# Wide attention of a Perceiver block: keys' high and low parts in tiles of their own, score products in row tiles, four chunks a step

## The reference, cut to what matters

```python
xn = _layernorm(x, ln_gamma, ln_beta)
q = (xn @ w_q).reshape(B, SQ, 16, 64)                 # B=4, SQ=256
k, v = split(context @ w_kv)                          # SK=4096, 16 heads of 64 each
scores = einsum('bqhd,bkhd->bhqk', q * 64**-0.5, k)
attn = softmax(scores, axis=-1)
out = einsum('bhqk,bkhd->bqhd', attn, v).reshape(B, SQ, 1024) @ w_out + b_out
```

## Time and profile before

| | |
|---|---|
| runs | 4200.05, 4213.23, 4216.68 us |
| profiled execution, span | 4206.0 us (the page gives no further time of it; the runs' median is 7.2 us above its span) |
| TensorE busy | 3714.7 us, 88% |
| VectorE, ScalarE, GpSimd busy | 2654.0, 2456.7, 1649.3 us |
| prelude of the wide attention | 73 to about 140 us |
| its loop | about 140 to 2080 us |
| granted TensorE clock | 0.943 of full speed over the span |

### The profile page before, as it was taken

One profiled execution on the slowest core, in us unless ns is written; L12 is line 12 of the kernel. 1 busy time (PEld: TensorE's weight loads), 2 busy tenths in 40 slices (PEclk: granted clock), 3 DMA queues, 4 the chain that ended last, 5 costly groups with the idle time before them and its releaser, 6 DMA issues. The chain is left out here.

```text
span 4206.0 us, 77561 instructions
## 1 busy us (share of the span) xinstructions
PE 3714.7 (88%) x28216; PEld 2624.0 (62%) x28216; DVE 2654.0 (63%) x3564; ACT 2456.7 (58%) x4550; POOL 1649.3 (39%) x1365
## 2 busy tenths in 40 slices
PE   5899999999999999999777895699999987767399
PEld 3677777777777777777454794555555543334298
DVE  4666666666666666666145412477878877467577
ACT  3677777776777777677424111266666666435165
POOL 2566666666666666666502201201111000014033
PEclk9999999999999999999788897799999999879599
DMA  6777677777767766665110384788887844100011
GB/s 217 269 253 248 239 260 257 254 249 257 249 243 256 257 245 224 230 223 211 63 36 6 138 319 168 236 165 179 178 166 178 160 77 65 25 11 1 17 46 44
DMA packets 236312, 727.25 MB, mean 173 GB/s; under 512 B 47884, under 2 KB 133132, under 8 KB 167052
## 3 DMA queue, kind: packets, MB, share of 16 engines
q1 hardware_dynamic: 233248, 713.89, 54.9%
q0 software_dynamic: 2688, 8.39, 0.5%
HBM read 627.80 MB, written 94.37 MB: 172 GB/s over the span
## 5 line engine op out<-in xcount | busy, mean ns | idle before, releaser
L753 POOL TENSOR_TENSOR wa_acc<-wa_acc,wa_probs 128x512 f32<-128x512 f32 x960 | 1246.7, 1299 | 527.8 <-ACT wa_probs L614 447.9
L678 DVE TENSOR_REDUCE wa_mx<-wa_ps_m 128x2 f32<-128x1024 f32 x512 | 626.8, 1224 | 487.2 <-PE wa_ps_m L489 487.1
L614 ACT ACTIVATE wa_probs<-wa_ps_s 128x512 f32<-128x512 f32 x1024 | 556.1, 595 | 530.9 <-PE wa_ps_s L535 525.6
L1292 DVE TENSOR_REDUCE na_mx<-na_ps_m 128x2 f32<-128x1024 f32 x512 | 613.8, 1220 | 196.1 <-PE na_ps_m L1113 192.6
L1237 ACT ACTIVATE na_probs<-na_ps_s 128x512 f32<-128x512 f32 x1024 | 555.8, 595 | 309.9 <-PE na_ps_s L1133 307.6
L606 ACT ACTIVATE wa_ps_s<-wa_m_wide 128x512 f32<-128x512 f32 x1024 | 575.5, 605 | 1.0
L511 PE MATMUL wa_ps_o<-wa_probs,wa_values 128*64 128x256 f32 x4096 | 507.6, 391 | 0.0
L450 PE MATMUL wa_ps_k<-wa_k_ctx,wa_w_k 128*128 128x512 f32 x1488 | 388.8, 397 | 0.0
L476 PE MATMUL wa_ps_v<-wa_w_v,wa_v_ctx 128*128 128x256 f32 x2880 | 383.1, 283 | 0.0
L535 PE MATMUL wa_ps_s<-wa_qh,wa_keys 128*128 128x256 f32 x2048 | 382.2, 309 | 0.0
L511 PEld LDWEIGHTS wa_ps_o<-wa_probs,wa_values 128*64 128x64 f32 x4096 | 275.3, 138 | 149.5 <-issue 7.5
(11 more groups left out here) (341 smaller groups left out, 5382.4 us busy)
## 6 DMA issues: line engine op xcount, KB each, us to landing
wa_k_ctx<-ctx_split SPq DMA_DIRECT2D x248, 1024.0 KB, 5.0
wa_v_ctx<-ctx_split SPq DMA_DIRECT2D x120, 1024.0 KB, 5.6
na_ctx<-ctx_split SPq DMA_DIRECT2D x56, 1024.0 KB, 11.8
na_keys<-k_rows SPq DMA_DIRECT2D x384, 128.0 KB
ctx_split<-wa_stage SPq DMA_DIRECT2D x32, 1024.0 KB, 9.7
wa_land<-in_ctxT SPq DMA_DIRECT2D x32, 512.0 KB, 10.0
ge_w_b<-in_w_rows SPq DMA_DIRECT2D x8, 2048.0 KB, 8.2
k_rows<-na_k_high SPq DMA_DIRECT2D x64, 256.0 KB, 3.3
```

Source lines behind the costliest of these rows:

```text
L614: act.activation(probs[:, c % R:c % R + 2, h * SQ:(h + 1) * SQ], ps_s[n % BANKS][:, :].rearrange("p (c n) -> p c n", c=2), ACT.Exp).then_i ...
L678: dve.tensor_reduce(mx[:, half, :, k], ps_m[:, :, :], AX.X, ALU.max).then_inc(m_taken, 1)
L753: pool.tensor_tensor(acc[:, :], acc[:, :], probs[:, c % R, :], ALU.add).then_inc(summed, 1)
L1292: dve.tensor_reduce(mx[:, half, :, k], ps_m[n % 2][:, :, :], AX.X, ALU.max).then_inc(m_taken, 1)
```

## The change

It touches `wide_attention` alone.

- `keys[i][h]` become `keys_high[i]` and `keys_low[i]`, both heads in their own 64 partitions; `qh` is kept once. `take_keys` is one 128-partition instruction on ScalarE and one on VectorE.
- All score products (low keys x high queries, high keys x high queries, high keys x low queries) are 64-row matmuls, head 0 and head 1 in turn: 24 a step.
- A step `j` is four chunks, eight steps a block. The score banks are four; the values' own bank is gone: in the loop value units go through the banks of the maxima (`ps_m[:, n, :]`), the turned maxima through `ps_m[:, 1, :]`, and in the prelude values go through the score banks.
- `acc` is doubled. `open_banks` comes after the prelude, with float32r matmuls.
- The order in a step is new for all streams:

```diff
+            for j in range(-2, LAST + 1):          # TensorE
+                a, st = j // SS, j % SS
+                of_max, kb, units = max_block(j), key_block(j), value_units(j)
+                if of_max is not None:
+                    pe.wait_ge(v_ready, values_before(j))
+                    if st == 0:
+                        pe.wait_ge(wide_ready, a + 1)
+                    maximum(*of_max, 0)
+                if 0 <= j < LAST:
+                    scores(2 * j)
+                    scores(2 * j + 1)
+                if of_max is not None:
+                    maximum(*of_max, 1)
+                if kb is not None:
+                    project_keys(kb)
+                if st == SS - 1 and a + 1 < G:
+                    pe.wait_ge(m_taken, maxima_through(j))
+                    turn_maximum(a + 1)
+                for n, (q, hb) in enumerate(units):
+                    pe.wait_ge(m_taken, maxima_through(j))
+                    pe.wait_ge(v_ready, values_before(j))
+                    if n and st == SS - 1 and a + 1 < G:
+                        pe.wait_ge(wide_ready, a + 2)
+                    project_values(q, hb, ps_m[:, n, :])
+                if j >= 1:
+                    weigh(j - 1)
+                if st == 0 and j > 0:
+                    denominator(a - 1)
...
+            for j in range(-2, LAST):              # ScalarE
+                turning = st == SS - 1 and a + 1 < G
+                kb = key_block(j)
+                if j >= 0:
+                    for n in range(4):
+                        exponents(4 * j + n)
+                if j >= -1 and not turning:
+                    initial(4 * j + 4)
                 if kb is not None:
                     take_keys(kb)
+                if turning:
+                    take_maximum(a + 1)
+                    initial(4 * j + 4)
+                if j >= -1:
+                    for n in range(1, 4):
+                        initial(4 * j + 4 + n)
+                if j >= 0 and st == 2 and a < BLOCKS - CG:
                     split(a + CG)
...
+            for j in range(-2, LAST + 2):          # VectorE
+                if st == SS - 1 and a + 1 < G:
+                    finish_maximum(a + 1)
+                if st == 1 and j > 1:
+                    copy_out(a - 1)
+                if of_max is not None:
+                    take_maximum(*of_max, 0)
+                    take_maximum(*of_max, 1)
+                if st == 1 and j > 1:
+                    divide(a - 1)
+                if j >= 0 and st == 2 and a < BLOCKS - CG:
+                    split_low(a + CG)
                 if kb is not None:
                     take_keys(kb)
+                for n, (q, hb) in enumerate(value_units(j)):
+                    take_values(q, hb, ps_m[:, n, :])
```

The score products and the schedule of value units:

```diff
             def scores(t):
...
+                    for n, (of, q) in enumerate(((keys_low, qh), (keys_high, qh), (keys_high, ql))):
+                        for h in range(2):
+                            r = slice(h * DH, (h + 1) * DH)
+                            ins = pe.matmul(ps_s[(2 * t + h) % BANKS][:, i * SQ:(i + 1) * SQ], of[a % 2][r, cols], q[a % 3][r, :],
+                                            start=False, stop=(n == 2), skip_group_check=True)
...
+        def max_block(j):
+            n = j + 1
+            return (1 + n // SS, n % SS) if 0 <= n < SS * (G - 1) else None
+        def value_units(j):
+            q, f = (j + 6) // (2 * SS), (j + 6) % (2 * SS)
+            if not 1 <= q < QUADS or f > 13:
+                return []
+            return [(q, hb) for hb in ((f,) if f < 12 else (2 * f - 12, 2 * f - 11))]
+        def values_before(j):
+            return 2 * CG + sum(len(value_units(i)) for i in range(-2, j))
```

More of the change, by code:

```diff
@@ L475, in project_values @@
                         for part, of in ((0, 0), (1, 0), (0, 1)):
-                            ins = pe.matmul(ps_v[:, i * 256:(i + 1) * 256], source[:, of, c, cols], w_v[:, part, c, :],
+                            ins = pe.matmul(bank[:, i * 256:(i + 1) * 256], source[:, of, c, cols], w_v[:, part, c, :],
                                             start=(n == 0), stop=(n == 3 * KD - 1))
@@ L488, in maximum @@
                     r = slice(h * DH, (h + 1) * DH)
-                    ins = pe.matmul(ps_m[:, h, :], qh[g % 3][r, h, half * P:(half + 1) * P],
-                                    keys[g % 2][h][r, k * 512:(k + 1) * 512], start=True, stop=True)
+                    ins = pe.matmul(ps_m[:, h, :], qh[g % 3][r, half * P:(half + 1) * P],
+                                    keys_high[g % 2][r, k * 512:(k + 1) * 512], start=True, stop=True)
                 ins.then_inc(m_done, 1)
@@ L498, in turn_maximum, with weigh @@
                         col = h * SQ + half * P
-                        ins = pe.matmul(ps_v[:, col:col + P], m_neg[:, 2 * half + h, :], ident[:, :], start=True, stop=True)
+                        ins = pe.matmul(ps_m[:, 1, col:col + P], m_neg[:, 2 * half + h, :], ident[:, :], start=True, stop=True)
                 ins.then_inc(mT_done, 1)
[L502 to L506, removed]
+            def weigh(j):
+                a, st = j // SS, j % SS
+                pe.wait_ge(exp_done, 4 * j + 4)
+                pe.wait_ge(v_ready, 2 * CG * (a // 2) + 2 * st + 2)
+                if st == 0 and a:
                     pe.wait_ge(o_copied, a)
-                for c in (2 * hb, 2 * hb + 1):
+                for c in range(4 * st, 4 * st + 4):
                     for h in range(2):
@@ L517, in denominator @@
                 for h in range(2):
-                    ins = pe.matmul(ps_o[h * DH:(h + 1) * DH, SQ:2 * SQ], ones[:, 0:DH], acc[:, h * SQ:(h + 1) * SQ],
+                    ins = pe.matmul(ps_o[h * DH:(h + 1) * DH, SQ:2 * SQ], ones[:, 0:DH], acc[a % 2][:, h * SQ:(h + 1) * SQ],
                                     start=True, stop=True)
@@ L549, in _ @@
             maximum(0, CG - 1, 1)
[L550 to L564, removed]
+            open_banks()
+            for j in range(-2, LAST + 1):
+                a, st = j // SS, j % SS
+                of_max, kb, units = max_block(j), key_block(j), value_units(j)
[9 more added lines that the diff above has]
+                    maximum(*of_max, 1)
                 if kb is not None:
                     project_keys(kb)
-                unit = value_unit(t)
-                if unit is not None:
-                    project_values(*unit, turns=(t + 1) // ST + 1)
+                if st == SS - 1 and a + 1 < G:
[11 more added lines that the diff above has]
+                    denominator(a - 1)
         @block.scalar
```

183 lines of the change are left out of this document (64 added, 119 removed).

## The result

The changed kernel takes 4266.9 us (median of four runs, 4263.35 to 4275.2), the kernel before 4206.64 us (four runs): ratio 1.0146, 95% interval 1.0124 to 1.0168, 60 us slower. Forecast were 4263 us and +50. That 4263 lies so near is in part luck: the 50 us were added to 4213, the median of three runs, and a fourth has brought the kernel before to 4206.64. The span of the profiled execution is 4273.4 us, 67 us longer; 60.3 us of these have come by the end of the wide attention's loop (its last denominators start 60.3 us later), the rest lies after it, where nothing was changed, and is less than the 12 us between this kernel's own runs.

The account below looks back on a forecast made before the run. The prediction took the wide attention's loop to be bound by TensorE's own order of work. Its terms, -12 - 13 - 5 + 62 + 18 = +50 us, added to 4213 gave 4263 us, range 4180 to 4315.

Parts of the forecast that it names:

- Tiling and switches: Wide attention's steps: score pairs still start 0.12 us apart, two tiling changes fewer save 0.39 us, 7.00 us a period.
- The chain through the banks: In a step, maxima and values wait for reductions in shared banks: 7.33 us a step, the 0.39 saved shrinks to 0.06.
- first link: In a step, the second maximum waits for the first reduction: 1.91 us after the first maximum instead of 1.76.
- Its second link: In a step, the values wait for the second reduction, to 3.82 us, where without waits they could start at 3.56.
- The values' first weights: In a step with values, the weight load of their first matmul is exposed: 0.10 us.
- Step 1: At a block's start, `copy_out` and `divide` on VectorE make the next step's first maximum 0.2 us later: 2 x 0.4 lost a pair.
- The split: Step 2, blocks 1 to 23: TensorE waits for values behind `split_low`, which waits for ScalarE: 2.65 us each, 62 with block 0.
- The clock: After half of the 23 gaps TensorE runs at its lower clock: 18 us; as a rival, every gap, about 4310, chance 0.14.
- Block 0: In the loop's first block, where no values are due, the maxima's reduction is late instead: 1.4 us.
- The last blocks: Last block of the loop: four chunks bound by GpSimd's adds at 5.2 to 5.5 us instead of 7.13, 13 us less.
- The prelude: Before the loop: one 512-column VectorE instruction less a round, 8 x 0.7 us, less 1 for the cold start: 5 us less.
- The faster rival: The reductions do not end last, 4182 us, or `split` does not hold the values, 4183 us; chance 0.22.

Follow-up runs that it names:

- the short reduction: Split first, with the maxima's reduction reading only the first 256 of each bank's 512 columns: 4083.6 us, ratio 0.9711 to the kernel before.
- split first: The changed kernel with ScalarE's `split` first in step 2, ahead of the exponents, instead of last: 4176.7 us, ratio 0.9932 to the kernel before.
- split_low later: The changed kernel with VectorE's `split_low` last in step 3 instead of before keys and values in step 2: 4180.7 us, 0.9942 to the kernel before.
- `copy_out` between the reductions: Split first, with `copy_out` between step 1's two reductions, reciprocal last in step 1, multiplication last in step 2: 4158.7 us, and 4156.4 us once more.

## Why the prediction was right, by its own steps

- Tiling and switches: right. Pairs go on at 0.12, a step without waits is 6.98 (7.00), shown by the short reduction. The rule of the Trainium skill weighed there ("TensorE: Matmul & The Clock Gate", "The mechanism") does not hold for these pairs: they follow each other at 0.12 us, though every matmul has a weight load of its own (3164 loads beside 3162 matmuls in the row of 800 to 1200 us) and both row groups are busy.
- The chain through the banks: right for its first link, the second maximum at 1.92 (1.91). Its second link does not bind: the values start at 3.86 (3.82), but 1.51 us behind the keys, and with the short reduction they start 1.50 behind them. The agreement there is luck. The chain costs a step the 0.26 us that I gave it (3.82 against 3.56), but by its first link alone: 0.15 of waiting before the second maximum and 0.11 behind it (keys 0.43 us later instead of 0.32). The values' first weights, for which I had another 0.10, cost nothing. So a step is 7.26, not 7.33. Step 1 lost more than the 0.4 I gave it: VectorE is 0.6 to 0.8 us late for step 2, and the maximum before waits 0.15. The two errors nearly cancel, luck again: 0.86 us a pair of blocks saved, 0.75 forecast.
- The split: right, and the step that decided. In blocks 1 to 23 the wait is 2.74 us in the mean (2.65 forecast), 63 us together (61). It is 2.40 in one half of them and 3.06 or more in the other; that `split_low` grows beside GpSimd's adds was not in the forecast. The clock: 17 of 23 gaps instead of half, but 1.2 us each instead of 1.5, so 21 us, not 18. Why six gaps of the same lengths left the clock up, no run shows. Block 0 was mis-sized: 5.8 us, not 1.4. All of it together is 90 us against 80.
- The last blocks: -13 forecast for the last one alone, -16.3 measured for two. The last block is 11.8 us shorter, and for the reason given: GpSimd adds without a break from its first add to its last, 1.41 us from one to the next, 5.65 per four chunks where I had 5.2 to 5.5. TensorE meanwhile goes at 4.2 us (below), since the ring of eight chunks lets GpSimd lag; the lag comes due at the end, when the last denominators wait 7.83 us for it. The block before it is 4.6 us shorter, which was not in the forecast.

```profile
2108.27 1.95 PE L509 MATMUL wa_ps_o<-wa_probs,wa_values 128*64 128x256 f32 x16
2112.47 1.95 PE L509 MATMUL wa_ps_o<-wa_probs,wa_values 128*64 128x256 f32 x16
...
2139.93 1.12 PE L516 MATMUL wa_ps_o<-wa_acc,g_ones 128*64 128x256 f32 x4 [7.83 <-POOL wa_acc L753]
```

- The prelude: wrong. -5 forecast; the first scores of block 0 come 0.7 us later (150.46, before 149.78). Its rounds are shorter, 5.5 to 5.7 us (keys at 97.11, 102.65, 108.38), but then ScalarE waits 7.7 us for a store of split context, TensorE idles 4.04 and goes on at half clock; and `open_banks`, 2.07 us, now stands between prelude and loop. In split first the first scores come at 148.48, in split_low later at 149.82, and in two runs of the same kernel (`copy_out` between the reductions) at 149.40 and 147.32: 2 us of it change from run to run. What share each cause has stays open.
- The sum: -13 for the steps (-12 forecast), -16 for the last blocks (-13), +1 for the prelude (-5) and +90 for the split with its clock (+80) give the 60 us but for 1. The miss of 10 is the prelude's 6 and block 0's 4; the smaller ones cancel.

The faster rival came true only as the kernel without the waits: the chain's first link is a limit, but the split alone decided the sign.

## What to carry to other kernels

When an engine's stream is reordered, look for every instruction that waits on the *end* of another engine's step, and ask what stands behind it: an in-order engine passes that wait on to work that has nothing to do with it. Here moving one call took 86 to 90 us off the changed kernel (4180.7 and 4176.7 us, by their ratios), some seven times the 13 us that the rest of the new order gained in blocks 1 to 29. Two uses of the same banks in one step put the reader's latency (0.55 + 1.22 + 0.14 us) on the writer's path, and a buffer doubled without need can shift an engine's work on top of another's.

## What the runs showed of the hardware

- A VectorE instruction with two inputs in SBUF that starts during one of GpSimd's adds is longer by what is left of the add, less some 0.15 us. The 128 x 256 multiplication, 0.42 us alone: started 0.28 us into an add of 1.28, it lasts 1.28; 0.71 into it, 0.86; 1.00 into it, 0.57. `split_low`, 1.23 alone, lasts 1.88 and 2.09 when it starts 0.48 and 0.28 into one. It goes the other way too: an add that starts while `split_low` has 0.94 us left lasts 2.07. The reciprocal (one input) stays at 1.74 to 1.75 in all of them, and reductions and copies from PSUM keep their times as well. The Trainium skill ("GPSIMD Engine Reference", "Specifications") names contention of VectorE instructions with two SBUF inputs; the traces agree and give it this price.
- This is why the second accumulator costs time. With it GpSimd's first add of a block comes 3.3 to 4.7 us before the denominators of the last block, with one 0.8 after them. The adds lie otherwise, and the multiplication meets one of them near its end instead of near its start. One block of the trace of split first shows it without an edit: in block 8 the multiplication starts between two adds and lasts 0.43, TensorE's wait of 0.6 us in step 2 is missing, and the block takes 60.99 us instead of 61.6.
- TensorE's gaps of 2.3 to 3.3 us, once a block, made the clock fall to its lower level in 17 of 23 cases, for 1.2 to 1.3 us of lost time each.
